# Reordering three steps inside the gated-linear-attention chunk loop of an 8-core transformer kernel

## The reference

```python
def _gla(h, Wq, Wk, Wv, Wg, Wo):
    q = _l2norm((h @ Wq).reshape(B, T, N_HEADS, D_K))      # 16 heads of 64
    k = _l2norm((h @ Wk).reshape(B, T, N_HEADS, D_K))
    v = (h @ Wv).reshape(B, T, N_HEADS, D_V)
    alpha = jax.nn.sigmoid(h @ Wg).reshape(B, T, N_HEADS, D_K)
    def step(S, inp):
        a_t, k_t, v_t, q_t = inp
        S = a_t[..., None] * S + k_t[..., None] * v_t[..., None, :]
        o_t = jnp.einsum('bhkv,bhk->bhv', S, q_t)
        return (S, o_t)
    ...
    return o @ Wo
h = _rmsnorm(x, g_attn);  x1 = x + _gla(h, Wq, Wk, Wv, Wg, Wo)
h = _rmsnorm(x1, g_ffn);  a = x1 + silu(h @ w1) * (h @ w2) @ w3
x = _layernorm(x + a)
# then, per group of 16 tokens: logits of 64 slots, an argmax mask, relu(sel @ f1 + bias) @ f2,
# scattered back with the mask, added to x, and a second layernorm
```

## Time and profile before

| | us |
|---|---|
| median of 3 runs | 6815.69 |
| the 3 runs | 6809.80 to 6817.64 |
| the profiled execution's own time | 6816.42 |
| its span, from the first instruction to the last (core 0, the slowest) | 6814.9 |
| spans of the 8 cores | 6745.0 to 6814.9 |

### The profile page before, as it was taken

The page is one execution under the profiler, slowest core; times in us unless marked ns, Lnnn a source line. Parts: engine busy times, 40 slices in busy tenths (PEclk is TensorE's granted clock), DMA queues, the critical chain, the costliest instruction groups (busy, mean ns, idle before and its releaser), DMA issues.

```text
span 6814.9 us, 80613 instructions; the slowest of 8 cores (6745.0 to 6814.9 us)
## 1 busy us (share of the span) xinstructions
PE 3659.4 (54%) x23296; PEld 2243.5 (33%) x23312; DVE 2617.3 (38%) x8166; ACT 1221.4 (18%) x4201; POOL 459.8 (7%) x796
## 2 busy tenths in 40 slices
PE   3554466555355545655535554665554555376553
PEld 2332245322233224532223332453222333255331
DVE  2444412354444441234444444113454444411455
ACT  2222211110222221011022222111102222111110
POOL 2000100000100010000010001000001000100000
PEclk8666588755666658875566665887556666598655
DMA  4000150144400015013340001401334000320223
GB/s 73 4 1 1 21 92 1 20 65 69 92 4 1 1 22 90 1 16 70 71 90 4 1 1 31 82 1 36 64 65 81 4 1 1 56 56 1 51 49 74
DMA packets 113924, 248.97 MB, mean 37 GB/s; under 512 B 12336, under 2 KB 12368, under 8 KB 113504
## 3 DMA queue, kind: packets, MB, share of 16 engines
q0 software_dynamic: 90464, 193.46, 16.9%
q1 hardware_dynamic: 23040, 50.34, 3.4%
HBM read 386.63 MB, written 16.78 MB: 59 GB/s over the span
## 4 chain that ended last, share of the span: by engine, by line
PE 42%; DVE 16%; DMA 14%; issue 14%; ACT 9%; POOL 2%; DVEq 1%; SPq 1%; ACTq 0%; another core or an unknown queue 0%; POOLq 0%
DMA SCb<-WA 5%; DMA WA<-f 4%; PE PA L382 4%; PE PB L382 3%; DMA WA<-w 2%; DVE SCb L634 2%; PE PDB L1036 2%; PE PC L1012 2%; PE PA L1012 2%; PE PA L789 2%; PE PB L789 1%; PE PG L1036 1%; DMA WA<-Wv 1%; PE PC L818 1%; PE PA L710 1%
## 5 line engine op out<-in xcount | busy, mean ns | idle before, releaser
L382 PE MATMUL PA<-YT,WA 128*128 128x256 bf16 x2048 | 346.3, 326 | 158.0 <-DVE YT L367 49.6
L382 PE MATMUL PB<-YT,WA 128*128 128x256 bf16 x2048 | 323.7, 311 | 69.0 <-ACT YT L393 42.5
L808 DVE TENSOR_TENSOR YT<-YT,PDB 128x256 bf16<-128x256 bf16 x96 | 40.5, 422 | 710.9 <-PE PDB L803 710.9
L680 DVE SCALAR_TENSOR_TENSOR STATE<-STATE,SFf 64x64 bf16<-64x64 bf16 x1024 | 287.4, 281 | 62.5 <-DVE SFf L675 1.4
L1043 DVE CAST WA<-PDB 64x512 bf16<-64x512 f32 x256 | 174.9, 683 | 345.8 <-PE PDB L1036 341.6
L382 PEld LDWEIGHTS PA<-YT,WA 128*128 128x128 bf16 x2048 | 218.2, 113 | 268.2 <-issue 217.3
L448 POOL TENSOR_TENSOR YT<-YT,SCb 128x256 bf16<-128x256 bf16 x256 | 166.0, 668 | 1985.9 <-ACT SCb L561 1688.7
L419 DVE TENSOR_SCALAR rows<-PS 16x256 f32<-16x256 f32 x32 | 11.9, 407 | 711.5 <-PE PS L410 711.5
L382 PEld LDWEIGHTS PB<-YT,WA 128*128 128x128 bf16 x2048 | 212.8, 109 | 171.9 <-issue 126.9
L263 POOL DMA_DIRECT2D WA<-f x128 | 68.2, 576 | 2432.6 <-DVE SCb L959 1070.7
L1036 PE MATMUL PDB<-WA,SCb 64*64 64x512 bf16 x256 | 160.6, 627 | 117.1 <-DMA WA<-f 108.0
(11 more groups left out here) (237 smaller groups left out, 8146.8 us busy)
## 6 DMA issues: line engine op xcount, KB each, us to landing
WA<-w POOLq DMA_DIRECT2D x64, 684.0 KB, 37.5
WA<-f POOLq DMA_DIRECT2D x128, 256.0 KB, 9.4
WA<-f POOLq DMA_DIRECT2D x16, 2048.0 KB, 22.2
SCb<-WA SPq DMA_DIRECT2D x256, 128.0 KB
WA<-w POOLq DMA_DIRECT2D x84, 256.0 KB, 52.3
XS<-x POOLq DMA_DIRECT2D x64, 256.0 KB, 7.5
y<-SFf SPq DMA_DIRECT2D x32, 512.0 KB
WA<-Wq POOLq DMA_DIRECT2D x32, 256.0 KB, 10.6
```

Of the source, the lines that this page charges most:

```text
L382: bld.emit("t", [lambda e, kc=kc, mc=mc, wn=wn, pt_=pt_, c0=c0: e.matmul(pt_[:, c0:c0 + 256], wsl(wn, kc, mc * 128, 128), YT[:, A_H + kc * ...
L680: e.scalar_tensor_tensor(STT_[p64(hh), doff + hh * 64:doff + (hh + 1) * 64], STT_[p64(hh), soff + hh * 64:soff + (hh + 1) * 64], SF[p64(hh ...
```

## The change

Two of the steps move inside the chunk loop; no instruction is added or taken away. Before, an iteration emits prep(cc+1), update(cc), the output matmuls of cc, tr(cc+2), the copy of the output of cc. After it, the order is tr(cc+2), update(cc), prep(cc+1), the output matmuls of cc, the copy of the output.

```diff
                     for cc in range(NC_T):
-                        if cc + 1 < NC_T:
-                            pregs[cc + 1] = gla_prep(cc + 1, trs[cc + 1])
+                        if cc + 2 < NC_T:
+                            trs[cc + 2] = gla_tr(cc + 2)
                         g = GP[cc % 2]
                         rkts, rvts, rvbd, rscm, rqg = pregs[cc]
...
                             reads=[rput, rcol, rsS], writes=[rdS])
+                        if cc + 1 < NC_T:
+                            pregs[cc + 1] = gla_prep(cc + 1, trs[cc + 1])
                         slo = rPB[g["pobn"]]
                         poc0 = (cc & 7) * 64
                         bld.emit("t", [
...
                         ], reads=[rvbd, rscm, rqg, rsS], writes=[slo])
-                        if cc + 2 < NC_T:
-                            trs[cc + 2] = gla_tr(cc + 2)
                         bld.emit("s", lambda e, hp=hp, cc=cc, g=g, poc0=poc0: e.copy(
```

## The result

The changed kernel takes 7029.84 us (median of 10 runs, 7011.85 to 7051.05), the one before 6814.07 (median of 10). The ratio is 1.031, with a 95% interval of 1.0289 to 1.033: slower by about 216 us, where 232 was forecast and the way was right. The profiled execution's span is 7024.2 us, 209.3 above the 6814.9 of before.

The account below looks back on a forecast made before the run. No engine is full, so the pair loop is a chain through the engines whose length goes into the time one for one. +2.10, +0.86, -0.27 and -0.88 make +1.81 us a pair, times 128 +232: 6816.4 to 7048 us, range 6990 to 7105.

Parts of the forecast that it names:

- Chunk 0, 3.24: First score-to-score interval of a pair: transposes, copies, update and state work before the mask, 3.24 us in place of 1.14.
- Chunk 1, 3.46: Second score-to-score interval: output first, then transposes, copies, update, state work and mask, 3.46 us in place of 2.60.
- chunk 2, 2.33: Third score-to-score interval: no transposes; output, update, state work and mask, 2.33 us in place of 2.60.
- Chunk 3, 3.12: Fourth interval, to the next pair's scores: output waits for L649, no longer for the state, 3.12 us in place of 4.00.
- The sum: The four intervals of a pair together: 12.15 us in place of 10.34, +1.81, times 128 pairs +232 us.
- L668 to L675: Step from the update's matmul on TensorE to the first state operation on VectorE: 0.43 us, bounds 0.37 and 0.46.
- What was called hidden: The output copy L700 and the KBD copy L598 (0.46 us) stay off the chain, both with over half a microsecond to spare.
- The stalls: Irregular delays in the pair loop, such as 0.73 us from L629 to L634; 0.11 us a pair, left unchanged.
- The rival that a wait on the own engine is free: VectorE's L675 to L680 takes 0.29 us, not 0.39; a pair 11.85, time 7009 us; chance 0.06.
- The rival that prep is not held: VectorE's L634 goes once L629 is done, not after the state work: 0.92 us less three times, 6695 us; chance 0.03.
- The rival of a longer hold: State work on VectorE delays prep longer, by upper bounds or stalls hitting more often: 7090 to 7110 us; chance 0.08.
- The rival without the wait for the copies: The update's wait for the new KTS and VTS copies is free or absent: +0.09 a pair, 6828 us; chance 0.05.

Follow-up runs that it names:

- own buffers: The changed kernel with separate KTS and VTS buffers for each of a pair's four chunks; 6815.4 us, ratio 0.9999 to the kernel before.
- the mask first: The changed kernel with L629 and the mask L634 issued between the update's matmuls and L675; 6758.6 us, ratio 0.9908 to the kernel before.
- the run without the wait for PUT: The changed kernel with two PUT buffers in turns, L680 reading the one written by the chunk before; 6949.4 us, ratio 1.0202 to the kernel before.
- prep alone moved: The kernel before with only prep(cc+1) moved behind the update, transposes left at the iteration's end; 6832.1 us, ratio 1.0024.
- the transposes alone moved: The kernel before with only tr(cc+2) moved to the iteration's head; 6742.1 us with separate KTS and VTS per chunk, 6743.5 us with shared ones.

## Why the prediction was right

Its steps, against the undisturbed intervals:

- The bound: the loop is a chain, its length goes into the time one for one. Held: +208.8 us in the loop, +0.5 elsewhere, clock 0.50 in all 16 passes before and after.
- Chunk 0, 3.24: measured 3.25. Both terms that make it, the wait for L621 and the hold of L634, are in the rows, and own buffers and the mask first each take one of them away.
- Chunk 1, 3.46, and chunk 2, 2.33: measured 3.36 and 2.23, 0.10 less each. One term was mis-sized. From L637 to the next matmul group I took 0.14, read where the update follows (163.63 to 163.77 in the earlier trace rows); the output follows at 0.02 to 0.03 (175.56 to 175.58 above). It is in both chunks.
- Chunk 3, 3.12: measured 3.13. The output waits for L649, not for the state.
- The sum: 12.15 a pair predicted, 11.97 measured, +1.63 in place of +1.81. Times 128 that is 209 us, the spans' 209.3. The 0.20 in chunks 1 and 2 is 26 us, the prediction's whole excess over the spans' difference, 232 - 209 = 23, and a little more. The medians are 216 apart, 7 more than the spans, in runs that scatter over 39 us; that the forecast looks closer against them is luck.
- L668 to L675, chosen at 0.43 between 0.37 and 0.46: measured 0.44 twice above (173.58 to 174.02, 176.94 to 177.38).
- What was called hidden: it is hidden, but with less to spare than the "over half a microsecond". The copy of KBD, 183.19 for 0.46, ends at 183.65 in the second pair, and VectorE's next operation on the path, the mask of prep(0), starts at 184.09, 0.44 later.
- The stalls: left as they were, 0.11 a pair, and the mean pair of the changed kernel is 12.08, again 0.11 over its 11.97.
- The rival that a wait on the own engine is free: refuted. By the Trainium skill, "VectorE: DVE Perf Modes", section "The DRAIN you can't avoid", eight chained copies took the same time with a semaphore after each as with one after the last. For the operations of 0.28 us here the run without the wait for PUT disagrees, by 0.19 us a wait; no run here tries it on longer ones. It is this rival's condition that fell, not the forecast, which had taken its durations from rows with the wait in them.
- The rival that prep is not held: refuted by L634 starting behind L680 in the rows above, and its size, 0.92, was 0.76 to 0.85 when the mask was issued first.
- The rival of a longer hold: not so. L634 starts 0.60 behind L680's start (174.41 to 175.01), where its bound was 0.70, and the stalls have not grown.
- The rival without the wait for the copies: not the case in the changed kernel; made true by own buffers, it gives 6815, where 6828 was worked out.

What the prediction did not see is that the two moves are not costly by themselves. The transposes' move alone gains 0.63 a pair, prep's alone loses 0.11, both together lose 1.63, so 2.15 comes from their meeting. Own buffers take 1.53 of that away. The remaining 0.62 is the transposes' gain, which is lost: with prep behind the state work, 10.44 with early transposes and own buffers is the same as the 10.45 with late ones. The mask behind the state work sets the interval there, so earlier copies are of no use. What is left of the transposes is their place ahead of an update in TensorE's order: it lengthens the first two intervals where they are early (2.48, 2.59, 2.24) and the second and third where they are late (2.14, 2.59, 2.59).

## What to carry to other kernels

When a step is moved ahead in a loop with two buffer sets, look at which buffers it writes: if a reader of this iteration stands behind the new writer, it gets a new wait (and other data), which may be free or cost the producer's whole path, depending on what stands between. In a chain of short operations, ask of each engine's order what stands ahead of the one operation for which another engine waits; putting the 0.3 us mask ahead of 1.0 us of state work that nobody waited for yet was worth 2.11 us a pair. Take each step's duration from a row with the same two neighbours, not from the nearest row alone; where there is none, as here for L637 and the output, one with the same two shapes was the better guide (L690 to L693, 0.04, against the 0.14 that was taken and the 0.02 that was measured).

## What the runs showed of the hardware

The step from one matmul's start to the next one's is short where the array shape that the row prints (128*128, 128*64 and so on) stays the same, and longer where it changes. All of this is at clock 0.50. With a full 128*128 before and after, a 64-column score matmul is followed at 0.02 to 0.03 us (L637 to L692 above), and L690 is followed by L693 at 0.04. When the shape changes it is more: L637 (128*128) to the transpose L608 (128*64) 0.14 (172.30 to 172.44), L668 (64*64) to L629 (64*128) 0.19, and the transpose to the update (128*64 to 64*64) 0.24 in the run with own buffers (173.82 to 174.06), where two transposes follow each other at 0.11. In the last case a part is length: a transpose has 128 columns, and two 64-column matmuls of one shape are 0.05 apart (L692 to L695 in the changed kernel) where two transposes are 0.11.

This last step explains the misses of the experiments. The expectations don't give their terms; if they took the 0.14 of L637 for it, it makes 0.10 of the 0.12 in the second and third interval of prep alone moved. In the transposes alone moved the matmul behind them is not the update but L629 (64*128), at 0.25 in the median, and that is most of the 0.17 in the first interval.

No run here varied the shape by itself, so that it is the shape, and not the operands or the PSUM bank, is argued and not shown.

On VectorE, an operation on 64 columns that waits for the one just ahead starts 0.39 after that one's start, and one that does not wait starts 0.20 after it: the two timelines with and without the wait for PUT.
